# New orders for the middle batches of a fused FFN, attention and FFN kernel: the last layer's second product in steps 6 to 9

## The chip, the cores and the metric

One core of one Trainium2 chip. The time is the device time of one execution in microseconds (us); before is the median of 3 runs. TensorE does matrix products, VectorE and ScalarE read its results from PSUM, GpSimd works on SBUF, SyncE (SP) issues transfers. Each engine runs its own list in order, and semaphores tie the lists together.

## The reference, cut to what matters

```python
x = x + 0.5 * ffn(layernorm(x))            # first FFN ("pre")
x = x + attention(layernorm(x))            # relu attention, and a layernorm of x + out
x = x + 0.5 * ffn(layernorm(x))            # last FFN ("post")

# ffn(x): h = layernorm(x) * gamma + beta; x + 0.5 * (silu(h @ w1 + b1) @ w2 + b2)
#   w1 (128 x 512) and w2 (512 x 128) are dequantised from integers
# attention(x): 16 heads of 8; w = relu(q @ k.T / sqrt(8)); w = w / (sum(w) + 1e-6); (w @ v) @ w_out + b_out
```

x is 8 batches x 512 tokens x 128 features, float32. All products are float32 (q with k as a float32r pair of high and low parts).

## The kernel before, in words

Attention sets the frame: each of the 8 batches has 16 steps (4 groups of 4 heads, by 4 tiles of 128 keys). A step's `step_scores` (S below, L648) writes four 128 x 512 score tiles into four PSUM banks, `scores[i][j]` in the order (0,0), (1,0), (0,1), (1,1). ScalarE takes the relu of i = 0 (L953), VectorE that of i = 1 (L1220), into `probs`, of which there are two sets. `step_values` of the step before (V below, L671) multiplies the relus into one of two `o_bank`s. S of the next step needs the four banks back, so it waits for all relus of this one. In the last batch ScalarE takes three of the four in the steps of THREE_BY_ACT, and in odd steps `scores[1][1]` is replaced by the bank of the pre stage.

Everything else is laid into these steps as fills, by lists written out by hand, one entry a step: PE_ORDER, ACT_ORDER, DVE_ORDER and POOL_ORDER for batches 1 to 6 (POOL_ORDER for 7 too), *_START for batch 0, *_END for batch 7, and *_FIRST and *_LAST around them. TensorE's entries have two parts: the early fills come between S and V, the late ones after V. GpSimd's list has no waits of its own for a step; only its order counts. A name is stage.work@offset, and offset is the batch relative to the one whose steps run: `pre...@1` is work for the next batch, `post...@-1` and `@-2` belong to batches whose attention is over. A name whose batch doesn't exist is left out by `tasks`; so in batch 1 there is no `@-2`.

Two stages, pre and post, have one PSUM bank each, `st.bank`, and each result must be read before the next fill may write it (`next_fill` waits for `st.free`). For a batch the pre bank takes hT (transposed rows), fc1.0 to fc1.3 (each 128 x 512, read by a Silu on ScalarE, L846), fc2 (four fills fc2.0 to fc2.3 that accumulate, read by VectorE as x1), uT, k, q and v. The post bank takes op (attention's output product, read as y), hT, fc1.0 to fc1.3, and fc2, read as out. Between them stand chains through VectorE and GpSimd: x1, x1_stats, x1_stats on GpSimd and u_apply lead to uT; oT.1, den.1, a.1 and aT to op; y, y_stats, y_apply, y_gamma, x2, x2_stats and x_apply to post.hT.

Of the kernel before, what the change touches and what calls it, by code (L numbers as in the profile page):

```python
# [37 lines left out]
POST_FILLS = ["hT", "fc1.0", "fc1.1", "fc1.2", "fc1.3", "fc2"]  # L38
# [28 lines left out]
    (["pre.hT@2"], []),  # L67
]
PE_ORDER = [
    ([], ["post.fc2.0@-2", "pre.fc1.0@1"]),  # L70
    (["post.fc2.1@-2", "post.fc2.2@-2", "post.fc2.3@-2", "pre.fc1.1@1"], []),
    (["pre.fc1.2@1", "post.op@-1"], []),
    (["pre.fc1.3@1"], []),
    (["pre.fc2.0@1"], []),
    ([], ["pre.fc2.1@1"]),
    (["pre.fc2.2@1", "pre.fc2.3@1"], []),
    ([], []),
    ([], []),
    ([], ["post.hT@-1"]),
    ([], []),  # L80
    ([], ["pre.uT@1", "post.fc1.0@-1"]),
    ([], ["pre.k@1", "post.fc1.1@-1"]),
    ([], ["pre.q@1", "post.fc1.2@-1"]),
    ([], ["pre.v@1"]),
    (["post.fc1.3@-1", "pre.hT@2"], []),
]

THREE_BY_ACT = (0, 1, 2, 3, 4, 8, 9, 10, 14)

PE_END = [  # L90
    ([], ["post.fc2.0@-2"]),
    (["post.fc2.1@-2", "post.fc2.2@-2", "post.fc2.3@-2"], []),
    ([], ["post.op@-1"]),
    ([], []),
    ([], []),
    ([], []),
    ([], []),
    ([], []),
    ([], []),
    ([], []),  # L100
# [36 lines left out]
ACT_ORDER = [  # L137
    ["pre.fc1.0@1"],
    ["pre.fc1.1@1"],
    ["pre.fc1.2@1", "post.store@-2", "pre.load_x@2"],  # L140
    ["pre.fc1.3@1"],
    ["post.y_apply@-1"],
    [],
    [],
    [],
    [],
    ["post.hT@-1"],
    [],
    ["pre.uT@1", "post.fc1.0@-1"],
    ["pre.k@1", "post.fc1.1@-1"],  # L150
    ["pre.q@1", "post.fc1.2@-1"],
    ["pre.v@1"],
    ["pre.hT@2", "post.fc1.3@-1"],
]
ACT_END = [
    [],
    [],
    ["post.store@-2"],
    [],
    [],  # L160
    [],
    ["post.y_apply@-1"],
    [],
    [],
    [],
    [],
# [32 lines left out]
]  # L199
DVE_ORDER = [  # L200
    ["oT.1@-1", "den.1@-1"],
    ["a.1@-1", "post.out@-2", "aT@-1"],
    ["post.y@-1", "post.y_stats@-1"],
    [],
    ["pre.x_stats@2"],
    ["post.x2@-1"],
    ["post.x2_stats@-1", "pre.x1@1"],
    [],
    ["pre.x1_stats@1"],
    [],  # L210
    [],
    [],
    ["oT.0", "den.0", "pre.k_lo@1"],
    ["pre.q_lo@1"],
    ["a.0"],
    [],
]
DVE_END = [
    [],
    ["oT.1@-1", "den.1@-1", "a.1@-1", "post.out@-2", "aT@-1"],  # L220
    ["post.y@-1"],
    [],
    ["post.y_stats@-1"],
    [],
    [],
    [],
    ["post.x2@-1"],
    ["post.x2_stats@-1"],
    ["oT.0"],
# [18 lines left out]
    "v_in.0@1", "v_in.1@1", "pre.x1_beta@1", "pre.xr@2"  # L248
]
POOL_ORDER = [  # L250
    [],
    ["post.u_bias"],
    ["post.y_stats@-1", "post.y_gamma@-1"],
    [],
    ["v_in.2", "post.x2_stats@-1", "post.x_apply@-1", "pre.x1_stats@1"],
    [],
    ["pre.u_apply@1"],
    ["pre.x_stats@2"],
    [],
    ["v_in.3", "pre.x_apply@2", "post.xr@-1"],  # L260
    [],
    ["v_in.0@1", "v_in.1@1"],
    ["pre.x1_beta@1"],
    [],
    ["pre.xr@2"],
    [],
]
# [35 lines left out]
def build(nc, x, w_qk, w_v, w_out, fc1_q, fc2_q, fc2_scales, columns, lines, out):  # L303
# [4 lines left out]
    with ExitStack() as ctx:  # L308
        def sb(name, shape, dtype=F32):
            return ctx.enter_context(nc.sbuf_tensor(name, shape, dtype))  # L310
# [4 lines left out]
        def sem(name):  # L315
            return ctx.enter_context(nc.semaphore(name))
# [66 lines left out]
        pre, post = Stage("pre", PRE_FILLS, 2), Stage("post", POST_FILLS, 1)  # L383
# [38 lines left out]
        def emptied(st, h, fill):  # L422

            if fill == "v":
                return pre.free, pre.n_at_edge(f"v.{h}")
            if fill == "q":
                return q_taken, 1
            if st is post and fill.startswith("fc1"):
                return last_silu, int(fill[-1]) + 1
            if st is post and h == 1:  # L430
                return last_free, ("hT", "fc2").index(fill) + 1
            if h == 1 or fill.startswith("fc1"):
                return st.free, len(st.fills) * (0 if st is pre else B - 1) + st.n_at_edge(fill)
            return st.free_a, st.n_at_edge(fill) - (FT if fill != "hT" else 0)

        def free_before(st, b, fill):

            return len(st.fills) * b + st.n(fill) - 1
# [22 lines left out]
        def fc1_bank(st, b, f):  # L461

            return scores[f // 2][:, f % 2, :] if st is post and b == B - 2 else st.bank[:, :]
# [10 lines left out]
        den, rec = sb("den", [P, QB, 2]), sb("rec", [P, QB, 2])  # L474
        a_t = sb("a_t", [P, QB, NP, 2, HD])
        aT = sb("aT", [P, S])
# [21 lines left out]
        v_in, v_in_a = sem("v_in"), sem("v_in_first_half")  # L498
# [8 lines left out]
        op_done, y_done = sem("op_done"), sem("y_done")  # L507
# [59 lines left out]
        def _(pe):  # L567
            mm, transpose = nc.tensor.matmul, nc.tensor.transpose

            def next_fill(st, b, fill):  # L570

                if free_before(st, b, fill) > 0:
                    pe.wait_ge(st.free, free_before(st, b, fill))
# [6 lines left out]
            def transposes(st, b, rows, done):  # L580

                pe.wait_ge(done, b + 1)
                for t in range(TT):
                    last = transpose(st.bank[:, P * t:P * (t + 1)], rows[:, t, :], ident[:, :])  # L584
                last.then_inc(st.full, 1)
# [8 lines left out]
            def by_columns(into, w, tokens):  # L594

                for j in range(HG):
                    part = slice(VW * j, VW * (j + 1))
                    last = mm(into[part, :], w[:, part], tokens, start=True, stop=True)  # L598
                return last

            def ffn(st, b, what):
                if what == "hT":
                    if st is pre and b == 1:

                        pe.wait_ge(*emptied(pre, 0, "v"))
                    else:
                        next_fill(st, b, "hT")
                    if st is post:
                        pe.wait_ge(y_done, b + 1)
                    transposes(st, b, st.h, st.rows)  # L610
                elif what.startswith("fc1"):
                    f = int(what[-1])
                    cols, into = slice(P * f, P * (f + 1)), fc1_bank(st, b, f)
                    if st is post and b == B - 2:

                        pe.wait_ge(probs_done[f // 2][f % 2], STEPS * B)
                        pe.wait_ge(post.free, len(POST_FILLS) * b + post.n("hT"))
                    else:
                        next_fill(st, b, what)
                    by_columns(into, w1_whole[:, cols], st.t[:, :]).then_inc(st.full, 1)  # L620
                elif what.startswith("fc2"):
                    f = int(what[-1])
                    if f == 0 and not (st is post and b == B - 2):
                        next_fill(st, b, "fc2")
                    pe.wait_ge(st.free, len(st.fills) * b + st.n(f"fc1.{f}"))
                    for t in range(TT):
                        last = by_tokens(st.bank, st.y[:, f, :], t, w2[:, f, :], f == 0 and t == 0, f == FT - 1 and t == TT - 1)
                    if f == FT - 1:
                        last.then_inc(st.full, 1)
# [45 lines left out]
            def task(stage, what, b):  # L675
                if stage == "pre":
                    per = len(PRE_FILLS)
                    if what == "uT":
                        next_fill(pre, b, "uT")
                        transposes(pre, b, u1, u_rows)  # L680
                    elif what in ("q", "k"):
                        i = "qk".index(what)
                        next_fill(pre, b, what)
                        by_columns(pre.bank[:, :], wqk[:, i, :], t_u[:, :]).then_inc(pre.full, 1)
                    elif what == "v":
                        pe.wait_ge(pre.free, per * b + pre.n("uT"))
                        next_fill(pre, b, "v")
                        for t in range(TT):
                            last = by_tokens(pre.bank, t_u, t, wv[:, :], True, True)
                        last.then_inc(pre.full, 1)  # L690
                    else:
                        ffn(pre, b, what)
                elif stage == "post":
                    if what == "op":
                        if b == 0:
                            pe.wait_ge(wo_loaded, 16)
                        pe.wait_ge(aT_in, b + 1)
                        if b > 0:

                            pe.wait_ge(post.free, len(POST_FILLS) * b)  # L700
                        for t in range(TT):
                            last = by_tokens(post.bank, aT, t, wo[:, :], True, True)
                        last.then_inc(op_done, 1)
                    else:
                        ffn(post, b, what)
# [746 lines left out]
```

## Time and profile before

| what | us |
|---|---|
| time, median of 3 runs (373.45 to 374.41) | 374.17 |
| the profiled execution: time, span | 373.73, 371.8 |
| TensorE busy | 362.6 (98%) |
| VectorE, ScalarE, GpSimd busy | 271.2, 228.4, 208.2 |
| granted TensorE clock | 1.000 |

Busy is a share of the span. A matmul that waits in the pipeline for a bank counts as busy, so lengths are better read as distances between starts.

### The profile page before, as it was taken

The numbers are of one execution on the slowest core, as the hardware profiler recorded it, in microseconds if no ns is written. First come the engines' busy times: TensorE is split into PE (matmuls) and PEld (weight loads), VectorE is DVE, ScalarE is ACT, GpSimd is POOL, SyncE is SP. The second block draws the span as 40 slices with busy tenths as digits, with TensorE's granted clock in tenths as the row PEclk, the third lists the DMA queues.
The fourth block names the chain that finished last, engine by engine and source line by source line (L and its number), as shares of the span: only waits on it lengthen the run. The fifth ranks groups of instructions, "written<-read, shape, count | busy, mean of one in ns | idle before, by whom it ended". The sixth has DMA issues, their size and how long they took to land.

```text
span 371.8 us, 12667 instructions
## 1 busy us (share of the span) xinstructions
PE 362.6 (98%) x5002; PEld 163.0 (44%) x5002; DVE 271.2 (73%) x666; ACT 228.4 (61%) x416; POOL 208.2 (56%) x440
## 2 busy tenths in 40 slices
PE   8989999999999999999999999999999999999996
PEld 7733423443364324453354433544345533532365
DVE  4766677896669966797767966789667777677673
ACT  3377466756756566556757567565665567588533
POOL 7495146458753697337781587535973384315541
PEclk9999999999999999999999999999999999999999
DMA  7016007300441016300271005410053001700001
GB/s 202 13 28 174 3 3 168 87 3 2 111 119 60 1 28 156 104 2 2 53 178 60 2 2 115 115 58 2 19 143 100 4 0 38 186 35 4 0 4 58
DMA packets 14105, 22.70 MB, mean 61 GB/s; under 512 B 2528, under 2 KB 3808, under 8 KB 14048
## 3 DMA queue, kind: packets, MB, share of 16 engines
q1 hardware_dynamic: 11456, 17.83, 19.8%
q10 hardware_dynamic: 2592, 4.07, 3.3%
q8 instruction: 40, 0.66, 0.7%
q14 instruction: 17, 0.14, 0.1%
HBM read 3.54 MB, written 2.10 MB: 15 GB/s over the span
## 4 chain that ended last, share of the span: by engine, by line
PE 92%; DVE 3%; ACT 2%; issue 2%; POOL 0%; POOLq 0%; DVEq 0%; ACTq 0%
PE o_bank L671 31%; PE scores L648 17%; PE pre_bank L598 10%; PE pre_bank L591 10%; PE post_bank L591 9%; PE post_bank L598 6%; PE scores L598 3%; PE pre_bank L584 2%; PE o_bank L578 2%; DVE probs L1220 1%; PE post_bank L584 1%; ACT probs L953 0%; ACT y_rows L881 0%; PE o_bank L598 0%; DVE post_x L1185 0%
## 5 line engine op out<-in xcount | busy, mean ns | idle before, releaser
L1220 DVE TENSOR_SCALAR probs<-scores 128x512 f32<-128x512 f32 x242 | 155.8, 683 | 59.4 <-PE scores L648 52.9
L953 ACT ACTIVATE probs<-scores 128x512 f32<-128x512 f32 x262 | 141.6, 595 | 64.0 <-PE scores L648 63.9
L671 PE MATMUL o_bank<-probs,v_op 128*32 128x512 f32 x1024 | 135.5, 601 | 0.3 <-DVE probs L1220 0.2
L648 PE MATMUL scores<-q_op,k_op 32*128 32x512 f32 x504 | 76.3, 495 | 1.1 <-ACT probs L953 0.6
L648 PEld LDWEIGHTS scores<-q_op,k_op 32*128 32x128 f32 x504 | 32.1, 181 | 95.3 <-issue 67.7
L671 PEld LDWEIGHTS o_bank<-probs,v_op 128*32 128x32 f32 x1024 | 23.4, 108 | 31.9 <-issue 30.7
L846 ACT ACTIVATE pre_y<-pre_bank,b_sum,col_consts 128x512 f32<-128x512 f32 x28 | 21.8, 779 | 22.9 <-PE pre_bank L598 22.9
L591 PE MATMUL pre_bank<-w,pre_y 128*32 128x128 f32 x960 | 30.7, 274 | 0.0
L598 PE MATMUL pre_bank<-pre_t,w_whole 128*32 128x512 f32 x224 | 29.5, 598 | 0.5 <-ACT pre_y L846 0.5
L591 PEld LDWEIGHTS pre_bank<-w,pre_y 128*32 128x32 f32 x960 | 25.8, 110 | 8.1 <-issue 7.6
L591 PE MATMUL post_bank<-w,post_y 128*32 128x128 f32 x960 | 29.3, 273 | 0.0
L591 PEld LDWEIGHTS post_bank<-w,post_y 128*32 128x32 f32 x960 | 26.2, 110 | 5.8 <-issue 5.3
L1322 POOL TENSOR_TENSOR v_op<-v_rows,v_op 128x128 f32<-128x128 f32 (+1 forms) x33 | 13.6, 423 | 24.5 <-ACT v_rows L867 24.5
L1249 POOL TENSOR_SCALAR norm_x_var<-norm_x_mv 128x4 f32<-128x4 f32 x21 | 4.2, 198 | 39.6 <-DVE norm_x_mv L1009 39.1
L1249 POOL TENSOR_SCALAR norm_y_var<-norm_y_mv 128x4 f32<-128x4 f32 x7 | 1.4, 199 | 43.8 <-DVE norm_y_mv L1009 43.8
L598 PE MATMUL post_bank<-post_t,w_whole 128*32 128x512 f32 x192 | 25.3, 598 | 0.0
L1252 POOL TENSOR_TENSOR norm_x_rs<-norm_x_var,minus_half 128x4 f32<-128x4 f32 x21 | 21.2, 1008 | 1.8
L846 ACT ACTIVATE post_y<-post_bank,b_sum,col_consts 128x512 f32<-128x512 f32 x24 | 18.7, 778 | 5.2 <-PE post_bank L598 5.2
L1383 POOL TENSOR_TENSOR y_rows<-y_rows,rows 128x512 f32<-128x512 f32 x7 | 9.1, 1293 | 16.3 <-ACT y_rows L881 14.2
L1289 POOL TENSOR_TENSOR norm_x_rs<-norm_x_var,minus_half 128x4 f32<-128x4 f32 x16 | 16.2, 1012 | 1.3
L1305 POOL TENSOR_SCALAR pre_xr<-pre_x,norm_x_mix 128x128 f32<-128x128 f32 x32 | 14.8, 476 | 0.8
L598 PE MATMUL pre_bank<-t_u,wqk 128*32 128x512 f32 x112 | 14.6, 594 | 0.1
(168 smaller groups left out, 437.3 us busy)
## 6 DMA issues: line engine op xcount, KB each, us to landing
k_op<-k_parts SPq DMA_DIRECT2D x62, 128.0 KB, 2.6
q_op<-q_parts SPq DMA_DIRECT2D x62, 128.0 KB, 2.8
out_dram<-o_rows ACTq DMA_DIRECT2D x7, 256.0 KB, 2.1
pre_x<-in_x_dram ACTq DMA_DIRECT2D x6, 256.0 KB, 3.1
w_int<-in_L_ffn_fc_q_dram SPq DMA_DIRECT2D x2, 256.0 KB, 4.2
rows<-in_lines_dram ACTq DMA_DIRECT2D x1, 256.0 KB, 6.6
s_rows<-in_L_ffn_fc_scales_dram SPq DMA_DIRECT2D x1, 256.0 KB, 7.5
wqk<-in_w_qk_dram SPq DMA_DIRECT2D x1, 256.0 KB, 7.6
```

What stands on the lines that cost most here:

```text
L584: last = transpose(st.bank[:, P * t:P * (t + 1)], rows[:, t, :], ident[:, :])
L591: last = mm(into[VW * j:VW * (j + 1), P * t:P * (t + 1)], tokens[:, part], w, start=start, stop=stop)
L598: last = mm(into[part, :], w[:, part], tokens, start=True, stop=True)
L648: mm(score_bank(b, s, i, j), k_op[rows, g, P * kt:P * (kt + 1)], q_op[rows, g, :], start=True, stop=True).then_inc(scores_done[i], 1)
L671: last = mm(o_bank[pair][VW * j:VW * (j + 1), :], v_op[:, kt, heads_of(g).start + 2 * j, :], probs[:, s % 2, j, :], start=(odd == 0 and kt ...
L846: activation(st.y[:, f, :], fc1_bank(st, b, f), ACT.Silu, bias=b1_sum[:, f:f + 1], scale=s1_col[:, f:f + 1]).then_inc(st.free, 1)
L953: activation(probs[:, s % 2, 2 * i + j, :], score_bank(b, s, i, j), ACT.Relu).then_inc(probs_done[i][j], 1)
L1220: v.tensor_scalar(probs[:, s % 2, 2 * i + j, :], score_bank(b, s, i, j), 0.0, None, ALU.max).then_inc(probs_done[i][j], 1)
L1252: p.tensor_tensor(norm.rs[:, i, :], norm.var[:, i, :], minus_half[:, i, :], ALU.pow).then_inc(norm.rs_in, 1)
L1289: p.tensor_tensor(norm.rs[:, 0, :], norm.var[:, 0, :], minus_half[:, 0, :], ALU.pow).then_inc(norm.half_in, 1)
L1305: last = p.tensor_scalar(st.xr[:, t, :], st.x(b)[:, t, :], norm.mix[:, 0, t:t + 1], norm.mix[:, 1, t:t + 1], ALU.mult, ALU.add)
L1322: return p.tensor_tensor(v_op[:, ts, heads, first:first + HD], rows, by_one, ALU.mult)
```

## The change

In batches 1 to 6 the four post.fc2@-2 fills go from steps 0 and 1 to steps 6 to 9, and the read of their result (out on VectorE) from step 1 to step 9, its store on ScalarE from step 2 to step 10. pre.fc2.1 goes from late in step 5 to late in step 4, and fc2.2 and fc2.3 from step 6 to step 5. uT goes from late in step 11 to early in step 10, k and q from late in steps 12 and 13 to early in steps 11 and 12, v from step 14 to 13. post.hT@-1 goes from step 9 to 10; post.fc1.0 to fc1.2 stay late in steps 11 to 13, post.fc1.3 goes from step 15 to 14, and hT@2 has step 15 to itself. On VectorE x2_stats, x1 and x1_stats go one step earlier, oT.0 and den.0 from step 12 to 8, a.0 from 14 to 10. In batch 7 post.op stays in step 2, and the fc2@-2 fills go from steps 0 and 1 to steps 3 to 6. GpSimd's list is ordered to match. post.fc2 now waits for y, since the op that shares its bank comes before it, and op waits for the last Silu of the batch before instead of for out.

```diff
 PE_ORDER = [
-    ([], ["post.fc2.0@-2", "pre.fc1.0@1"]),
-    (["post.fc2.1@-2", "post.fc2.2@-2", "post.fc2.3@-2", "pre.fc1.1@1"], []),
+    ([], ["pre.fc1.0@1"]),
+    (["pre.fc1.1@1"], []),
     (["pre.fc1.2@1", "post.op@-1"], []),
     (["pre.fc1.3@1"], []),
-    (["pre.fc2.0@1"], []),
-    ([], ["pre.fc2.1@1"]),
+    (["pre.fc2.0@1"], ["pre.fc2.1@1"]),
     (["pre.fc2.2@1", "pre.fc2.3@1"], []),
-    ([], []),
-    ([], []),
-    ([], ["post.hT@-1"]),
-    ([], []),
-    ([], ["pre.uT@1", "post.fc1.0@-1"]),
-    ([], ["pre.k@1", "post.fc1.1@-1"]),
-    ([], ["pre.q@1", "post.fc1.2@-1"]),
-    ([], ["pre.v@1"]),
-    (["post.fc1.3@-1", "pre.hT@2"], []),
+    ([], ["post.fc2.0@-2"]),
+    ([], ["post.fc2.1@-2"]),
+    ([], ["post.fc2.2@-2"]),
+    (["post.fc2.3@-2"], []),
+    (["pre.uT@1"], ["post.hT@-1"]),
+    (["pre.k@1"], ["post.fc1.0@-1"]),
+    (["pre.q@1"], ["post.fc1.1@-1"]),
+    ([], ["pre.v@1", "post.fc1.2@-1"]),
+    (["post.fc1.3@-1"], []),
+    (["pre.hT@2"], []),
 ]
 PE_END = [
-    ([], ["post.fc2.0@-2"]),
-    (["post.fc2.1@-2", "post.fc2.2@-2", "post.fc2.3@-2"], []),
-    ([], ["post.op@-1"]),
-    ([], []),
-    ([], []),
     ([], []),
     ([], []),
+    ([], ["post.op@-1"]),
+    ([], ["post.fc2.0@-2"]),
+    ([], ["post.fc2.1@-2"]),
+    ([], ["post.fc2.2@-2"]),
+    (["post.fc2.3@-2"], []),
...
 DVE_ORDER = [
     ["oT.1@-1", "den.1@-1"],
-    ["a.1@-1", "post.out@-2", "aT@-1"],
+    ["a.1@-1", "aT@-1"],
     ["post.y@-1", "post.y_stats@-1"],
     [],
     ["pre.x_stats@2"],
-    ["post.x2@-1"],
-    ["post.x2_stats@-1", "pre.x1@1"],
-    [],
+    ["post.x2@-1", "post.x2_stats@-1"],
+    ["pre.x1@1"],
     ["pre.x1_stats@1"],
-    [],
-    [],
-    [],
-    ["oT.0", "den.0", "pre.k_lo@1"],
+    ["oT.0", "den.0"],
+    ["post.out@-2"],
+    ["a.0"],
+    ["pre.k_lo@1"],
     ["pre.q_lo@1"],
-    ["a.0"],
+    [],
+    [],
     [],
 ]
...
                     if f == 0 and not (st is post and b == B - 2):
                         next_fill(st, b, "fc2")
+                        if st is post:
+
+                            pe.wait_ge(y_done, b + 2)
...
-                            pe.wait_ge(post.free, len(POST_FILLS) * b)
+                            pe.wait_ge(post.free, len(POST_FILLS) * (b - 1) + post.n("fc1.3"))
```

## Rows read from the trace of the kernel before

**Rows 1.** The page, part 4: the chain that ended last, by engine.

```profile
PE 92%; DVE 3%; ACT 2%; issue 2%; POOL 0%; POOLq 0%; DVEq 0%; ACTq 0%
```

**Rows 2.** Timeline, TensorE, batch 1: start, length, instructions, [idle before and releaser].

```profile
60.42 0.50 PE L648 MATMUL scores<-q_op,k_op 32*128 32x512 f32 x4
...
62.71 0.51 PE L648 MATMUL scores<-q_op,k_op 32*128 32x512 f32 x4
63.68 1.06 PE L598 MATMUL pre_bank<-pre_t,w_whole 128*32 128x512 f32 x8 [0.46 <-ACT pre_y L846]
...
65.53 0.51 PE L648 MATMUL scores<-q_op,k_op 32*128 32x512 f32 x4
...
68.70 0.51 PE L648 MATMUL scores<-q_op,k_op 32*128 32x512 f32 x4
...
70.99 0.72 PE L648 MATMUL scores<-q_op,k_op 32*128 32x512 f32 x4
...
73.51 0.51 PE L648 MATMUL scores<-q_op,k_op 32*128 32x512 f32 x4
...
82.40 0.51 PE L648 MATMUL scores<-q_op,k_op 32*128 32x512 f32 x4
82.84 1.06 PE L671 MATMUL o_bank<-probs,v_op 128*32 128x512 f32 x8
83.83 0.66 PE L584 MATMUL post_bank<-ident,post_h 128*128 128x128 f32 x4
84.42 0.85 PE L648 MATMUL scores<-q_op,k_op 32*128 32x512 f32 x4
85.20 1.07 PE L671 MATMUL o_bank<-probs,v_op 128*32 128x512 f32 x8
...
101.01 0.51 PE L648 MATMUL scores<-q_op,k_op 32*128 32x512 f32 x4
```

**Rows 3.** Timeline, VectorE, batch 1.

```profile
61.07 1.29 DVE L1220 TENSOR_SCALAR probs<-scores 128x512 f32<-128x512 f32 x2 [1.19 <-PE scores L648]
...
63.50 1.22 DVE L1220 TENSOR_SCALAR probs<-scores 128x512 f32<-128x512 f32 x2
64.64 0.41 DVE L1028 TENSOR_TENSOR a_t<-o_t,rec 128x256 f32<-128x256 f32 x1
65.09 0.71 DVE L1034 STREAM_TRANSPOSE aT<-a_t 128x512 f32<-128x512 f32 x1
...
75.68 0.90 DVE L1074 TENSOR_TENSOR post_x<-y_rows,x_beta 128x512 f32<-128x512 f32 x1 [0.25 <-POOL y_rows L1383]
76.50 1.28 DVE L1220 TENSOR_SCALAR probs<-scores 128x512 f32<-128x512 f32 x2
77.70 0.85 DVE L1000 BATCH_NORM_STATS2 norm_x_stats<-post_x 128x6 f32<-128x128 f32 x4
...
78.89 0.66 DVE L1046 TENSOR_TENSOR x<-pre_bank,pre_xr 128x512 f32<-128x512 f32 x1
79.63 2.72 DVE L1220 TENSOR_SCALAR probs<-scores 128x512 f32<-128x512 f32 x4
82.27 0.86 DVE L1000 BATCH_NORM_STATS2 norm_x_stats<-x 128x6 f32<-128x128 f32 x4
...
83.47 1.25 DVE L1220 TENSOR_SCALAR probs<-scores 128x512 f32<-128x512 f32 x2
```

**Rows 4.** Timeline, GpSimd, batch 1: the last step of u_apply.

```profile
85.67 1.76 POOL L1280 TENSOR_SCALAR u<-x,norm_x_rs,norm_x_shift 128x128 f32<-128x128 f32 x4 [0.21 <-POOL norm_x_shift L1256]
```

**Rows 5.** Timeline, TensorE: first scores of batches 6 and 7; step 6 and V(7) of batch 7.

```profile
275.22 0.50 PE L648 MATMUL scores<-q_op,k_op 32*128 32x512 f32 x4
...
318.25 0.51 PE L648 MATMUL scores<-q_op,k_op 32*128 32x512 f32 x4
...
331.69 0.76 PE L648 MATMUL scores<-q_op,k_op 32*128 32x512 f32 x4
...
336.33 1.06 PE L671 MATMUL o_bank<-probs,v_op 128*32 128x512 f32 x8
```

More of the change, by code:

```diff
@@ L139 @@
     ["pre.fc1.1@1"],
-    ["pre.fc1.2@1", "post.store@-2", "pre.load_x@2"],
+    ["pre.fc1.2@1", "pre.load_x@2"],
     ["pre.fc1.3@1"],
@@ L146 @@
     [],
-    ["post.hT@-1"],
     [],
[L149 to L153, printed above, removed]
+    ["post.store@-2", "pre.uT@1", "post.hT@-1"],
+    ["pre.k@1", "post.fc1.0@-1"],
+    ["pre.q@1", "post.fc1.1@-1"],
+    ["pre.v@1", "post.fc1.2@-1"],
+    ["post.fc1.3@-1"],
+    ["pre.hT@2"],
 ]
@@ L157 @@
     [],
-    ["post.store@-2"],
+    [],
     [],
@@ L162 @@
     ["post.y_apply@-1"],
-    [],
+    ["post.store@-2"],
     [],
@@ L205 @@
     ["pre.x_stats@2"],
-    ["post.x2@-1"],
-    ["post.x2_stats@-1", "pre.x1@1"],
-    [],
+    ["post.x2@-1", "post.x2_stats@-1"],
+    ["pre.x1@1"],
     ["pre.x1_stats@1"],
-    [],
-    [],
-    [],
-    ["oT.0", "den.0", "pre.k_lo@1"],
-    ["pre.q_lo@1"],
-    ["a.0"],
+    ["oT.0", "den.0"],
+    ["post.out@-2"],
+    ["a.0"],
+    ["pre.k_lo@1"],
+    ["pre.q_lo@1"],
+    [],
+    [],
     [],
@@ L219 @@
     [],
-    ["oT.1@-1", "den.1@-1", "a.1@-1", "post.out@-2", "aT@-1"],
+    ["oT.1@-1", "den.1@-1", "a.1@-1", "aT@-1"],
     ["post.y@-1"],
@@ L225 @@
     [],
-    [],
+    ["post.out@-2"],
     ["post.x2@-1"],
@@ L250 @@
 POOL_ORDER = [
-    [],
+    ["v_in.2"],
     ["post.u_bias"],
@@ L254 @@
     [],
-    ["v_in.2", "post.x2_stats@-1", "post.x_apply@-1", "pre.x1_stats@1"],
     [],
-    ["pre.u_apply@1"],
     ["pre.x_stats@2"],
-    [],
-    ["v_in.3", "pre.x_apply@2", "post.xr@-1"],
+    ["post.x2_stats@-1", "post.x_apply@-1", "v_in.3"],
+    ["pre.x1_stats@1", "pre.u_apply@1"],
+    [],
+    ["pre.x_apply@2"],
+    ["post.xr@-1"],
     [],
+    ["pre.x1_beta@1"],
     ["v_in.0@1", "v_in.1@1"],
-    ["pre.x1_beta@1"],
-    [],
     ["pre.xr@2"],
```

## The prediction

> **What bounds the kernel now.** I read the chain that ended last first: nine tenths of the span is TensorE, so what counts is the order and the gaps of TensorE's stream [rows 1]. The busy share says little about gaps, because a score matmul that waits for its PSUM bank is drawn long and counts as busy. So I read TensorE's timeline and take every length as the distance from one start to the next [rows 2]; batch 1 holds every pattern that the change uses.
> A step is S (four score matmuls), V (eight value matmuls) and its fills. S takes 0.44 (82.40 to 82.84), V alone 0.99 (to 83.83), a turn ("hT", "uT") 0.59 (to 84.42), a step with one fill 2.29 (68.70 to 70.99), with two 3.17 (65.53 to 68.70); so one more fill is 0.88 [rows 2]. Early or late in the step costs TensorE the same.
> Two things stretch this. (a) The last score matmul takes the bank that VectorE's second relu has read: in batch 1's step 10 that relu ends at 83.47 + 1.25 = 84.72 and V starts at 85.20, 0.48 later [rows 2, 3]. (b) Each stage has one bank for its fills: in step 1 fc1.1 starts 0.97 after S (62.71 to 63.68) instead of 0.44, released by the Silu of fc1.0, a late fill of the step before; step 1 is 2.82 [rows 2]. In the later batches of before the three post.fc2 fills stand between the two, and cover that wait.
> VectorE's own pace: its relus start 0.65 after S (60.42 to 61.07), a pair ends after 1.28 but makes room for the next instruction after 1.20 (76.50 to 77.70); x2_stats 1.19, x1 0.74, x1_stats 1.20, x2 0.82 (75.68 to 76.50), oT with den 63.50 - 61.07 - 1.20 = 1.23, a 0.45, aT 0.71 [rows 3].
>
> **The change, a middle batch (2 to 5).** No instruction is added or dropped; only orders and two waits that are met long before (y_done for post.fc2, and the op wait, which now asks for the Silu of fc1.3 instead of out). SP's list and the DMAs are unchanged; the store moves to step 10 on ScalarE, behind its relus, and ScalarE has room for it. What counts is how long the steps are in the new order.
> Steps 0 to 3 now read exactly as batch 1's do in before, where post.fc2 does not exist: 70.99 - 60.42 = 10.57 [rows 2], wait (b) of 0.53 included; it used to be hidden. Step 4: as 70.99 to 73.51, 2.52 (VectorE's y and y_stats are the same neighbours, so their 0.22 wait stays), plus fc2.1, 0.88: 3.40. So step 5 starts at T = 13.97. Step 5 has two fills, 3.17; steps 6 to 9 one each, 9.16; so the uT of step 10 can start at T + 12.77 (with S). Step 10 then takes 0.59 + 0.99 + 0.59 = 2.17, steps 11 to 13 two fills each, 9.51. Step 14 has fc1.3 early behind fc1.2 late in step 13: wait (b) again, since it is the same pair on the other stage's bank, so 2.82. Step 15 is 0.44 + 0.59 + 0.99 = 2.02. Sum 13.97 + 12.77 + 2.17 + 9.51 + 2.82 + 2.02 = 43.26. Before, batches 2 to 5 took (275.22 - 101.01) / 4 = 43.55 [rows 2, 5]. Gain 0.29 each, 1.16 for four: the stalls in the empty steps 7, 8 and 10 go, and two waits of 0.53 come.
> Does VectorE keep up? After relu(5) it is free at T + 0.65 + 1.20 = T + 1.85; x2 to 2.67, x2_stats 3.86, relu(6) 5.06, x1 5.80. relu(7) waits for its scores until T + 6.11, free 7.31; x1_stats 8.51; relu(8) 9.71; oT.0 and den.0 10.94; relu(9) ends 12.22, and 0.48 on is 12.70: in time for 12.77, with 0.07 to spare. out, a.0, k_lo and q_lo lie in steps with 0.4 or more to spare.
> Does GpSimd? u's last apply ends at 85.67 + 1.76 = 87.43, 5.16 after x1_stats starts at 82.27 [rows 3, 4]. Here x1_stats starts at T + 7.31, so u is there at T + 12.47, 0.30 before uT.
> These are narrow, and no row shows this neighbourhood. From below the cost is zero, from above 0.3 a batch (that the last hand-over falls behind by as much as its spare). I take 0.1, nearer the rows, for each of batches 1 to 6: 0.5 to 0.6 in all.
>
> **Batch 1** is in the middle table too, but its post.fc2@-2 does not exist: steps 6 to 9 are empty, four in a row, where before only 7, 8 and 10 were. There VectorE sets the pace, one piece behind the other: relu(6) to 5.06, x1 5.80, relu(7) 7.00, x1_stats 8.20, relu(8) 9.40, oT.0 and den.0 10.63, relu(9) ends 11.91, + 0.48 = T + 12.39. So the batch takes 43.26 - 0.38 = 42.88, though TensorE has four fills less to do; before it took 101.01 - 60.42 = 40.59 [rows 2]. Loss 2.29. This is the largest term: before, those fills sat in steps 0 and 1, whose length was TensorE's own, so leaving them out shortened the batch; now they sit where VectorE's work (oT.0 and den.0 moved up from step 12) fills the time anyway.
>
> **Batch 6** has no hT@2: its step 15 is empty, 1.43. 42.67 against 318.25 - 275.22 = 43.03 [rows 5]: gain 0.36.
>
> **Batch 7.** From its first S (Z). relu(15) ended 1.93 after S(15), so V(15) starts 0.48 later, at Z + 0.98, and S(1) at Z + 1.97. VectorE does one relu there (free at Z + 3.22), then oT.1 with den.1, a.1 and aT: 1.23 + 0.45 + 0.71, ending at Z + 5.61. op in step 2 needs aT, and TensorE is there by Z + 4.7 to 5.2 (the three fills that covered this chain in step 1 are gone), so it waits and starts at 5.65; behind it wait the scores of step 3, and so both relu engines. S(3) at 6.62, three one-fill steps, S(6) at 13.49. In step 6 y_apply delays ScalarE's relus: V(7) starts 336.33 - 331.69 = 4.64 after S(6), so Z + 18.13, against 336.33 - 318.25 = 18.08 before [rows 5]. The fill in step 6 now hides what the wait at op costs: +0.05. Bounds -0.5 and +1.0, since which of the three relus of ScalarE ends last in steps 0 to 2 is no row here. The tail is the same.
>
> **Sum.** 2.29 - 1.16 - 0.36 + 0.05 = +0.82, with the 0.1 a batch for tight hand-overs +1.4; I take +1.3. The profiled execution has 373.73 us for its span of 371.8, so 375.0; it lay 0.44 under the median of 374.17, which gives 375.5 for the median.
>
> **A page against the rows.** The Trainium skill, VectorE: DVE Perf Modes, section "The DRAIN you can't avoid", says that the next VectorE operation does not start until the pipe of the last is empty. The row of a relu pair is 1.28 long and its follower starts after 1.20 [rows 3]; the trace does not agree, so the sum goes by start distances.
>
> **Rivals.** (1) Faster: wait (b) does not come. If the Silu of a late fill freed the bank before S is over, step 14 of batches 1 to 6 and step 1 of batches 2 to 6 would be 0.53 shorter, 11 x 0.53 = 5.8, and the time 369.7. It decides from about 5 of the 11: then the time falls below 373.1. For it: in before no middle batch shows the wait. Against: there nothing asks for the bank so soon, and the one place that does shows it [rows 2]. Chance 0.12, with a smaller loss in batch 1 in it.
> (2) VectorE's chain or u runs late in all middle batches: the 0.07 and 0.30 are used up, den takes longer beside GpSimd. 0.3 to 0.5 for each of batches 2 to 6: 377.3. For it: the spare is less than a tenth of one relu pair. Against: each duration repeats in before. Chance 0.2. To it belongs what the full-length spacing would do as a mechanism: follower 0.08 later for each of four relu pairs is 0.3 in batch 1 and 0.25 in each of five others, +1.6, 377.1; this is what the page's rule would bring; chance 0.03 of the 0.2.
> (3) Nothing to see: batch 1 loses its 2.29, but the others gain 0.4 to 0.5, and no tight hand-over costs anything: 374.2. Chance 0.13.
> The forecast has 0.55, and its own range is 374.6 to 376.4.
>
> **How the numbers follow.** 0.3%, 1.12 us, is about what a measurement of this kernel can tell from no change, so slower begins at 375.3. The forecast lies close above it: of its 0.55 I give 0.33 to slower, 0.22 to the same. With rival 2 slower has 0.53, with rival 3 the same 0.35, faster 0.12. The range 374.0 to 377.3 leaves out most of rival 1 and the ends of 2 and of batch 7's bound.
>
> **What would show it.** Batch 1 near 43 from first S to first S, batches 2 to 5 near 43.3; in them fc1.1 of step 1 and fc1.3 of step 14 released by a Silu 0.97 after S; S(7) to S(10) of batch 1 drawn 0.7 to 1.2 long behind VectorE's relu; op of batch 7 released by aT. It is wrong if batch 1 stays near 41, or if middle batches come under 42.8 or over 43.7.

## The result and the profile after

The changed kernel takes 375.0 us (median of 13 runs, 374.21 to 375.75), the kernel before 373.87 beside it (13 runs, 373.4 to 374.42): ratio 1.0031, 95% interval 1.0022 to 1.0040. It is slower by 0.2 to 0.4%; the forecast of 375.5 was 0.5 too high, its direction right. As a difference the forecast was +1.3, and +1.13 was measured. The profiled execution has a span of 373.1 us against 371.8.

The chain that ended last has less TensorE and more of what TensorE waits for:

```profile
PE 86%; DVE 6%; ACT 3%; issue 2%; DMA 1%; POOL 0%; SPq 0%; ACTq 0%; DVEq 0%; POOLq 0%
```

The timeline of TensorE in batch 1, in the same columns as [rows 2]:

```profile
60.46 0.51 PE L651 MATMUL scores<-q_op,k_op 32*128 32x512 f32 x4 [0.50 <-DMA q_op<-q_parts]
...
62.75 0.51 PE L651 MATMUL scores<-q_op,k_op 32*128 32x512 f32 x4
63.72 1.07 PE L598 MATMUL pre_bank<-pre_t,w_whole 128*32 128x512 f32 x8 [0.46 <-ACT pre_y L849]
...
71.04 0.73 PE L651 MATMUL scores<-q_op,k_op 32*128 32x512 f32 x4
...
74.44 0.51 PE L651 MATMUL scores<-q_op,k_op 32*128 32x512 f32 x4
...
79.05 1.05 PE L651 MATMUL scores<-q_op,k_op 32*128 32x512 f32 x4
...
81.02 0.86 PE L651 MATMUL scores<-q_op,k_op 32*128 32x512 f32 x4
...
82.81 1.45 PE L651 MATMUL scores<-q_op,k_op 32*128 32x512 f32 x4
...
85.19 1.44 PE L651 MATMUL scores<-q_op,k_op 32*128 32x512 f32 x4
86.57 0.64 PE L584 MATMUL pre_bank<-ident,u 128*128 128x128 f32 x4
...
98.17 0.51 PE L651 MATMUL scores<-q_op,k_op 32*128 32x512 f32 x4
99.14 1.07 PE L598 MATMUL post_bank<-post_t,w_whole 128*32 128x512 f32 x8 [0.46 <-ACT post_y L849]
...
101.00 0.50 PE L651 MATMUL scores<-q_op,k_op 32*128 32x512 f32 x4
...
103.01 0.51 PE L651 MATMUL scores<-q_op,k_op 32*128 32x512 f32 x4
```

The reader is to see three things. The batch takes 103.01 - 60.46 = 42.55, where it took 40.59 [rows 2]. Four scores in a row, from 79.05 on, are drawn 0.86 to 1.45 long where 0.5 is normal: TensorE waits in steps 7 to 10, behind VectorE's relus (steps 6 to 9 have no fill). And two fills are released by a Silu, each 0.97 after its S: fc1.1 at 63.72 and, new, fc1.3 of the post stage at 99.14, which makes step 14 101.00 - 98.17 = 2.83 long.

VectorE and GpSimd in the same stretch, to be held against [rows 3, 4]:

```profile
76.27 0.68 DVE L1077 TENSOR_TENSOR post_x<-y_rows,x_beta 128x512 f32<-128x512 f32 x1
76.99 0.87 DVE L1003 BATCH_NORM_STATS2 norm_x_stats<-post_x 128x6 f32<-128x128 f32 x4
...
79.46 0.68 DVE L1049 TENSOR_TENSOR x<-pre_bank,pre_xr 128x512 f32<-128x512 f32 x1
80.06 1.28 DVE L1223 TENSOR_SCALAR probs<-scores 128x512 f32<-128x512 f32 x2
81.25 0.86 DVE L1003 BATCH_NORM_STATS2 norm_x_stats<-x 128x6 f32<-128x128 f32 x4
82.15 0.38 DVE L1012 BATCH_NORM_AGGREGATE norm_x_mv<-norm_x_stats 128x2 f32<-128x6 f32 x4
82.45 1.26 DVE L1223 TENSOR_SCALAR probs<-scores 128x512 f32<-128x512 f32 x2
83.62 0.71 DVE L1021 STREAM_TRANSPOSE o_t<-o_bank 128x512 f32<-128x512 f32 x1
84.36 0.19 DVE L1024 TENSOR_SCALAR den<-o_t 128x32 f32<-128x32 f32 x1
84.59 0.35 DVE L1026 RECIPROCAL rec<-den 128x32 f32<-128x32 f32 x1
84.86 2.58 DVE L1223 TENSOR_SCALAR probs<-scores 128x512 f32<-128x512 f32 x4
```

```profile
84.66 1.76 POOL L1283 TENSOR_SCALAR u<-x,norm_x_rs,norm_x_shift 128x128 f32<-128x128 f32 x4 [0.21 <-POOL norm_x_shift L1259]
```

VectorE has no gap: relu(9) starts at 84.86 (the row holds two pairs, 1.29 each) and ends 1.29 later, and 0.48 on is 86.63; uT starts at 86.57. But u too is ready only at 84.66 + 1.76 = 86.42. Two chains end within 0.2 of each other.

All batches, from first S to first S (each a difference of such rows; the last column is from batch 7's first S to its last):

| kernel | batch 1 | 2 to 5, each | 6 | 7 to last S |
|---|---|---|---|---|
| before | 40.59 | 43.54 to 43.57 | 43.03 | 29.59 |
| changed | 42.55 | 43.24 to 43.28 | 42.67 | 30.46 |
| difference in all | +1.96 | -1.16 | -0.36 | +0.87 |

That is +1.31; the spans differ by 1.3. Two more differences of these two executions cancel. The first S of all starts at 21.45 instead of 21.92, and batch 0, whose lists are the same in both kernels, takes 39.01 instead of 38.50, since the first S of batch 1 waits 0.50 for the transfer of q_op (the row at 60.46). Of the twelve traces five have this wait, 0.31 to 0.60 long, and seven do not; what decides it is open. The tail, from the last S to the end, is 23.91 against 23.96.

Batch 7: VectorE ahead of op, and ScalarE around the store, then the scores that wait (TensorE):

```profile
323.78 0.71 DVE L1037 STREAM_TRANSPOSE aT<-a_t 128x512 f32<-128x512 f32 x1
```

```profile
335.58 1.07 ACT L956 ACTIVATE probs<-scores 128x512 f32<-128x512 f32 x2
337.34 0.34 ACTq L889 DMA_DIRECT2D out_dram<-o_rows  x1
337.78 2.56 ACT L956 ACTIVATE probs<-scores 128x512 f32<-128x512 f32 x5 [1.13 <-DVE o_rows L1087]
```

```profile
318.73 1.06 PE L651 MATMUL scores<-q_op,k_op 32*128 32x512 f32 x4
...
324.54 1.08 PE L591 MATMUL post_bank<-wo,aT 128*32 128x128 f32 x32 [0.45 <-DVE aT L1037]
...
337.13 1.07 PE L674 MATMUL o_bank<-probs,v_op 128*32 128x512 f32 x8
338.43 0.98 PE L651 MATMUL scores<-q_op,k_op 32*128 32x512 f32 x3 [0.23 <-ACT probs L956]
```

op waits for aT, as foretold. What was not foretold is the 1.13 before ScalarE's relus of step 8: its list has the store in step 7, the store waits for out, and out is behind VectorE's relus.

### The profile page after: what moved, and what is told of

Read it like the earlier page. It is cut to its first block, busy times and chain, and to the rows that moved or that the text cites. A ratio compares the mean times of both kernels' runs of the same rounds, so it can differ in the third digit from the quotient of the medians.

```text
span 373.1 us, 12667 instructions
## 1 busy us (share of the span) xinstructions
PE 358.3 (96%) x5002; PEld 161.3 (43%) x5002; DVE 268.8 (72%) x666; ACT 228.4 (61%) x416; POOL 208.4 (56%) x440
## 3 DMA queue, kind: packets, MB, share of 16 engines
HBM read 3.54 MB, written 2.10 MB: 15 GB/s over the span
## 4 chain that ended last, share of the span: by engine, by line
PE 86%; DVE 6%; ACT 3%; issue 2%; DMA 1%; POOL 0%; SPq 0%; ACTq 0%; DVEq 0%; POOLq 0%
PE o_bank L674 28%; PE scores L651 13%; PE pre_bank L598 11%; PE pre_bank L591 10%; PE post_bank L591 9%; PE post_bank L598 6%; PE scores L598 3%; DVE probs L1223 3%; PE pre_bank L584 2%; PE o_bank L578 2%; ACT pre_y L849 1%; ACT post_y L849 1%; PE post_bank L584 1%; DMA q_op<-q_parts 1%; DVE o_t L1021 1%
## 5 line engine op out<-in xcount | busy, mean ns | idle before, releaser
L651 PE MATMUL scores<-q_op,k_op 32*128 32x512 f32 x504 | 72.9, 495 | 1.4 <-DMA q_op<-q_parts 0.5
L651 PEld LDWEIGHTS scores<-q_op,k_op 32*128 32x128 f32 x504 | 29.2, 181 | 88.2 <-issue 71.0
L674 PEld LDWEIGHTS o_bank<-probs,v_op 128*32 128x32 f32 x1024 | 25.5, 109 | 36.3 <-issue 33.5
L591 PE MATMUL post_bank<-w,post_y 128*32 128x128 f32 x960 | 31.5, 273 | 0.0
```

Source lines behind the costliest of these rows:

```text
L591: last = mm(into[VW * j:VW * (j + 1), P * t:P * (t + 1)], tokens[:, part], w, start=start, stop=stop)
L651: mm(score_bank(b, s, i, j), k_op[rows, g, P * kt:P * (kt + 1)], q_op[rows, g, :], start=True, stop=True).then_inc(scores_done[i], 1)
L674: last = mm(o_bank[pair][VW * j:VW * (j + 1), :], v_op[:, kt, heads_of(g).start + 2 * j, :], probs[:, s % 2, j, :], start=(odd == 0 and kt ...
```

## The experiments

Ratios are to the kernel before on the same chip. The parts act in different batches, so the trace tells them apart better than the time does.

**Batch 1 in the order of before.**

```diff
+PE_SECOND, ACT_SECOND, DVE_SECOND, POOL_SECOND = the four lists of the kernel before
-def of_batch(b, start, order, end):
-    return start if b == 0 else end if b == B - 1 else order
+def of_batch(b, start, second, order, end):
+    return start if b == 0 else second if b == 1 else end if b == B - 1 else order
...
-            for beside in POOL_ORDER:
+            for beside in POOL_SECOND if b == 1 else POOL_ORDER:
```

> Batch 1 alone gets the order lists of the kernel before; all else is the changed kernel. Theory: in batch 1 the moved fills do not exist, and steps 6 to 9 run at VectorE's pace; the trace of the changed kernel has 42.55 us from the first S of batch 1 to that of batch 2, before had 40.59. So batch 1 returns to 40.6 and the time falls by 1.96, from 375.0 to 373.0, which is 0.8 under before (373.87). Rival: the batch is long for what comes into it from batch 0 (q and k transfers, values), not for its own order; then the time stays within 0.5 of 375.0. Rival 2: the time saved is waited for again in batch 2; then batch 2 grows above 43.25.

Measured 373.08 us, ratio 0.9988 (0.9976 to 1.0000). Its first scores of batches 1 and 2 (TensorE):

```profile
60.35 0.50 PE L724 MATMUL scores<-q_op,k_op 32*128 32x512 f32 x4
...
100.94 0.51 PE L724 MATMUL scores<-q_op,k_op 32*128 32x512 f32 x4
```

Batch 1 takes 40.59 again, and batches 2 to 6 keep their 43.23 to 43.28 and 42.65. The loss is batch 1's own order. By the trace the middle order alone is a gain of 1.5 in batches 2 to 6; the time is only 0.5 under before, since batch 7 keeps its loss.

**Batch 7 in the order of before.**

```diff
 (PE_END, ACT_END and DVE_END of the kernel before)
-                        if st is post:
+                        if st is post and b < B - 3:
                             pe.wait_ge(y_done, b + 2)
...
-                            pe.wait_ge(post.free, len(POST_FILLS) * (b - 1) + post.n("fc1.3"))
+                            pe.wait_ge(post.free, len(POST_FILLS) * (b if b == B - 2 else b - 1)
+                                       + (0 if b == B - 2 else post.n("fc1.3")))
```

> Batch 7 alone gets the lists of before, with the two waits that belong to that order. In the changed kernel its last S comes 30.47 us after its first, before 29.60. Theory: the order of batch 7 is worth 0.87 (wait for aT at op, and the store), so 374.1. Rival: the long first S (0.99) that comes from batch 6's empty last step makes the loss; batch 7 keeps it in this run, so the time would fall by less than 0.4.

Measured 374.59, ratio 1.0029 (1.0018 to 1.0040). Batch 7 takes 30.14 to its last S, 0.32 less than in the changed kernel, not 0.87. The rival holds: batch 7's first S waits in this kernel too (V 0.98 after S, as in the changed kernel 0.99), because batch 6 now ends in an empty step.

```profile
318.73 1.04 PE L651 MATMUL scores<-q_op,k_op 32*128 32x512 f32 x4
319.71 1.06 PE L674 MATMUL o_bank<-probs,v_op 128*32 128x512 f32 x8
```

So 0.87 splits: 0.55 by that first S, which belongs to the order of batch 6, and 0.32 by batch 7's own order.

**The store one step later.**

```diff
 ACT_END = [
...
     ["post.y_apply@-1"],
-    ["post.store@-2"],
     [],
+    ["post.store@-2"],
```

> In batch 7 the store of out goes from step 7 to step 8 of ScalarE's list. In the changed kernel ScalarE's relus of step 8 start 1.13 late, released by VectorE's out; V(8) and the steps behind it are late. Theory: the wait in front of the store costs the 0.5 that batch 7 lost between V(7) and its last S (12.06 against 11.52 before), so 374.5. Rival: out itself takes VectorE's time before relu(8); then nothing changes, 375.0.

Measured 374.43, ratio 1.0020 (1.0010 to 1.0030), which overlaps the changed kernel's; the trace decides. ScalarE no longer stops:

```profile
335.72 1.07 ACT L956 ACTIVATE probs<-scores 128x512 f32<-128x512 f32 x2
337.02 0.60 ACT L956 ACTIVATE probs<-scores 128x512 f32<-128x512 f32 x1 [0.23 <-PE scores L651]
```

The gap of 1.13 is 0.23, and batch 7 takes 29.89 instead of 30.46. So the place of the store costs 0.57. With it out of the way the new order of batch 7 is 0.25 better than the old one of the experiment above (30.14); 0.57 less 0.25 is the 0.32 found there.

**op in step 3 of batch 7** (with the store later).

```diff
 PE_END = [
     ([], []),
     ([], []),
-    ([], ["post.op@-1"]),
-    ([], ["post.fc2.0@-2"]),
+    ([], []),
+    ([], ["post.op@-1"]),
+    ([], ["post.fc2.0@-2"]),
...
 (fc2.1 to fc2.3 and y one step later, out behind x2, the store one step later)
```

> The changed kernel with the store later, and in batch 7 op in step 3 instead of 2, fc2@-2 in steps 4 to 7, y one step later, out and the store after x2. Theory: op in step 2 waits 0.62 for aT, with the scores and both relu engines behind it; in step 3 aT is there, so batch 7 goes from 29.89 to 29.3 and the time to 373.8. Rival: y, y_apply and x2 are late then, and a later step takes it back; 374.4 or more.

Measured 374.63, ratio 1.0022 (1.0010 to 1.0034); batch 7 takes 30.03, against 29.89 with op in step 2. The time is in the rival's range, but not for its reason. op no longer waits, but S of step 3 does:

```profile
324.37 0.50 PE L651 MATMUL scores<-q_op,k_op 32*128 32x512 f32 x1
325.46 0.50 PE L651 MATMUL scores<-q_op,k_op 32*128 32x512 f32 x2 [0.59 <-DVE probs L1223]
```

VectorE's one relu of step 2 is queued behind oT.1, den.1, a.1 and aT. The 2.4 us of VectorE work stayed in its empty step, and a wait for VectorE stayed too, at S instead of at op. That the wait would go with this work was not tried.

**fc1.3 late in step 14.**

```diff
-    (["post.fc1.3@-1"], []),
+    ([], ["post.fc1.3@-1"]),
     (["pre.hT@2"], []),
```

> post.fc1.3@-1 goes from early to late in step 14 of batches 1 to 6, nothing else. Theory of the one bank: early, it waits for the Silu of fc1.2 until 0.97 after S; late, it starts 1.32 after S, when the bank is free. Step 14 goes from 2.82 to 2.29, six times 0.53 = 3.2: 371.8. Rival: the Silu is then later and ScalarE's relus of step 15 or the copy of hT come late; S of step 0 or fc1.0 takes back up to 0.5 a batch, and the time stays within 1 of 375.0.

Measured 371.60, ratio 0.9948 (0.9936 to 0.9960). TensorE in batch 3, steps 14 and 15:

```profile
183.06 0.50 PE L651 MATMUL scores<-q_op,k_op 32*128 32x512 f32 x4
183.49 1.07 PE L674 MATMUL o_bank<-probs,v_op 128*32 128x512 f32 x8
184.37 1.04 PE L598 MATMUL post_bank<-post_t,w_whole 128*32 128x512 f32 x8
185.34 0.51 PE L651 MATMUL scores<-q_op,k_op 32*128 32x512 f32 x4
```

The step is 2.28, and the middle batches 42.71 to 42.74: the 0.53 is gone in each and nothing takes it back. (Batch 6, with its empty last step, falls by 0.40, and the first step of batch 7 by 0.13.) One entry moved from the early to the late side of the same step is worth 3 us, and makes this kernel faster than before by 0.4 to 0.6%.

**The other fills late too.**

```diff
     ([], ["pre.fc1.0@1"]),
-    (["pre.fc1.1@1"], []),
-    (["pre.fc1.2@1", "post.op@-1"], []),
-    (["pre.fc1.3@1"], []),
-    (["pre.fc2.0@1"], ["pre.fc2.1@1"]),
+    ([], ["pre.fc1.1@1"]),
+    ([], ["post.op@-1", "pre.fc1.2@1"]),
+    ([], ["pre.fc1.3@1"]),
+    ([], ["pre.fc2.0@1", "pre.fc2.1@1"]),
```

> Batches 1 to 6: besides post.fc1.3 (step 14), pre.fc1.1, fc1.2, fc1.3 and fc2.0 go from early to late in steps 1 to 4, op goes ahead of fc1.2. Theory of the one bank: step 1 loses its 0.53 wait as step 14 did, and with op later in step 2 VectorE's y no longer... delays relu(3), or still does: y can start 0.3 after relu(2) instead of 0.5 behind it, and S(4) keeps 0 to 0.22 of its wait. So 0.53 x 6 more than fc1.3 alone, and up to 0.22 x 6: 371.6 - 3.2 - 0.7 = 367.7, between 367.1 and 368.4; middle batches 42.0 to 42.2. Rival: with all fills late VectorE's chain (0.07 spare at step 10) or ScalarE's Silus, which now come before each relu pair, become the bound and give back 0.3 or more a batch: over 369.5.

Measured 370.41, ratio 0.9906 (0.9889 to 0.9922): a miss for the theory, and in the rival's range, though the wait that takes the gain back is not one that the rival names. Step 1 lost its 0.53, but the middle batches came down by 0.16 only, to 42.55 to 42.58. S(4) keeps its 0.22, since y_stats still stands ahead of relu(3), and S(2) is 0.38 over. VectorE's den.1 is 0.83 long here. The lines of VectorE and GpSimd (batch 3, step 0):

```profile
148.40 0.83 DVE L1024 TENSOR_SCALAR den<-o_t 128x32 f32<-128x32 f32 x1
149.26 0.35 DVE L1026 RECIPROCAL rec<-den 128x32 f32<-128x32 f32 x1
149.53 1.22 DVE L1223 TENSOR_SCALAR probs<-scores 128x512 f32<-128x512 f32 x2
```

```profile
147.51 0.42 POOL L1325 TENSOR_TENSOR v_op<-v_rows,v_op 128x128 f32<-128x128 f32 x1
147.89 1.28 POOL L1377 TENSOR_TENSOR u_bias<-u,rows 128x512 f32<-128x512 f32 x1
```

den should take 0.19; it ends at 149.23, when GpSimd's u_bias (149.17) has ended. In the changed kernel it meets only the end of u_bias in these batches, and takes 0.28 to 0.31.

**oT.0 and den.0 back to step 12, in batch 1 alone.**

```diff
+DVE_SECOND = DVE_ORDER with oT.0, den.0 in step 12 and a.0 in step 14, for b == 1
```

> The changed kernel, but in batch 1 alone oT.0 and den.0 go back from step 8 to step 12 and a.0 to step 14. VectorE's chain from step 5 to relu(9) is then 1.2 shorter. If that chain alone sets when step 10's uT starts, batch 1 falls from 42.55 to 41.3 and the time by 1.2. If u sets it nearly as much (in the changed kernel GpSimd's last u ends at 86.42 and uT starts at 86.57), the wait only moves from S to uT and batch 1 falls by 0.1 to 0.2: 374.8.

Measured 374.68, ratio 1.0020 (1.0011 to 1.0030), and in the trace batch 1 is 42.51 instead of 42.55. TensorE at step 10:

```profile
84.45 0.50 PE L670 MATMUL scores<-q_op,k_op 32*128 32x512 f32 x4
85.82 0.63 PE L603 MATMUL pre_bank<-ident,u 128*128 128x128 f32 x4 [0.86 <-POOL u L1302]
```

VectorE's chain, which my prediction gave as the cause, is 1.1 to 1.2 shorter, and the batch is as long: the wait now carries u's name. The two are nearly equal bounds, and taking one away shows the other. What is common to both is x1_stats: VectorE starts it 20.79 after the batch's first S in the changed kernel (at 81.25) and 20.78 after it here. That an earlier x1_stats would shorten the batch is argued, not shown.

**All together.** Batch 1 as before with its fc1 and fc2.0 fills late, late fills in batches 2 to 6, the store later.

```diff
 (the edits above: the late fills, the lists of before for b == 1 with theirs late, the store)
```

> All at once: late fills in batches 2 to 6, in batch 1 the order of before with fc1 and fc2.0 late, the store of batch 7 one step later. Theory: the parts add, since each acts in its own batch or step: batch 1 39.9, batches 2 to 5 42.0 each, batch 6 41.4, batch 7 29.9 to its last S; 365.3. Rival: the parts share their gain (the next bound in a batch comes up); over 367.

Measured 368.07, ratio 0.9839 (0.9825 to 0.9854). Batch 1 is 40.05, batches 2 to 5 42.54 to 42.59, batch 6 42.09, batch 7 29.73. The parts add: batch 1 is the 40.59 of the order of before less the 0.54 of fc1.1's wait, the middle batches are those of the kernel with late fills, and batch 7 is 0.55 shorter than there, as with the store alone. The time is over the rival's 367, but not because parts share their gain: the 365.3 that I expected had 42.0 for a middle batch, without den's wait and S(4)'s.

**GpSimd out of den's way.**

```diff
 POOL_ORDER = [
     ["v_in.2"],
-    ["post.u_bias"],
+    [],
...
-    ["post.xr@-1"],
+    ["post.xr@-1", "pre.xr@2"],
     [],
     ["pre.x1_beta@1"],
-    ["v_in.0@1", "v_in.1@1"],
-    ["pre.xr@2"],
+    ["v_in.0@1", "v_in.1@1", "post.u_bias@1"],
+    [],
 (batch 1's list likewise, with x1_beta ahead of v_in.0 and v_in.1; its own u_bias stays in step 1)
```

> The combined kernel, with GpSimd's list alone changed: xr@2 right behind xr@-1, and u_bias of the next batch right behind v_in.1@1, so that GpSimd is idle when VectorE does den.1 in step 0. In the combined kernel den.1 takes 0.82 to 0.83 in batches 2 to 6 instead of 0.19, and ends as GpSimd's u_bias ends; relu(1) is late and S of step 2 is 0.38 long over. Theory: den waits for GpSimd's instruction; with GpSimd idle it takes 0.2, S(2) comes down to 0.44 to 0.49, and five batches lose 0.35 each: 368.1 - 1.8 = 366.3. Rival: den waits for something else (the result of the transpose, the semaphore); den stays at 0.8 and the time within 0.5 of 368.1. Rival 2: the earlier xr delays v_in.0 or x1_beta, and V(0) or x1 waits: over 368.

Measured 366.92, ratio 0.9810 (0.9794 to 0.9826). GpSimd is idle from 185.44 to 194.86, and VectorE's den.1 of batch 4 in that stretch:

```profile
188.31 0.19 DVE L1097 TENSOR_SCALAR den<-o_t 128x32 f32<-128x32 f32 x1
```

den waits for GpSimd's instruction: with GpSimd idle it takes 0.19. Batches 2 to 5 take 42.17 to 42.21, 0.34 to 0.40 less. The time fell by 1.15 and not by 1.8, because of batch 1. GpSimd's list is still full there at that place, and the same thing happened to another operation. VectorE, then GpSimd:

```profile
64.87 1.40 DVE L1104 TENSOR_TENSOR a_t<-o_t,rec 128x256 f32<-128x256 f32 x1
```

```profile
64.70 1.28 POOL L1391 TENSOR_TENSOR pre_xr<-pre_xr,b_quarter 128x512 f32<-128x512 f32 x1
```

a.1 takes 0.41 when alone. It cost 0.63 at op, and batch 1 is 40.70 here. In the combined kernel a.1 begins at 64.03, ahead of the same instruction of GpSimd at 64.30, and takes 0.46. The order turned because TensorE's first S of batch 1 waited for q_op's transfer here (0.32) and not there. In all five traces with that wait a.1 takes 1.02 to 1.41, in the other seven 0.41 to 0.46.

**y_stats one step later.**

```diff
 DVE_ORDER = [
...
-    ["post.y@-1", "post.y_stats@-1"],
-    [],
+    ["post.y@-1"],
+    ["post.y_stats@-1"],
```

> As the kernel with GpSimd's list changed, and y_stats goes from step 2 to step 3 of VectorE's list, behind relu(3), in batches 1 to 6. Theory: relu(3) no longer waits behind y_stats, and S(4) loses its 0.22: six times, 1.3 less, 365.0. Rival: y_stats is 1.7 later; y_apply then meets relu(5) on ScalarE and y_gamma comes after relu(5) on VectorE, so x2 and the chain behind it, which has 0.07 to 0.1 to spare, run late and give back 0.2 to 0.4 a batch: 366.0 to 367.5.

Measured 368.81, ratio 0.9869 (0.9855 to 0.9884): a miss for the theory. S(4) lost its 0.22, and S(7) now waits 0.42, since x2 and the chain behind it are late; middle batches take 42.39 to 42.41, 0.2 more than without the move. The rival was right in kind. The time went up by 1.9. Of this the traces show 1.0 in batches 2 to 6 (0.2 each), 0.7 in batch 1 (41.41 against 40.70) and 0.3 in batch 0, whose end waits 0.60 for q_op's transfer instead of 0.32.

## Why the prediction was right

Point by point, by its own steps.

- Middle batches: computed 43.26, measured 43.24 to 43.28. The starts read in batch 1 of before, put together in the new order, are right to 0.02. Both waits of kind (b), at fc1.1 and fc1.3, came 0.97 after S, and the experiment with fc1.3 late showed that the one bank is the cause. The rival that this wait does not come (369.7) is out.
- The 0.1 a batch for narrow hand-overs did not exist: nothing was late. This term, 0.5 of the forecast, was wrong. The spare was also larger than the 0.07 computed, since x2 takes 0.72 in the new order and not 0.82.
- Batch 1: loss 2.29 computed, 1.96 measured. uT started at 86.57 - 74.44 = 12.13 after T instead of 12.39. The size was off because VectorE's x2 and x1 took less room there (76.99 - 76.27 = 0.72 and 80.06 - 79.46 = 0.60) than the 0.82 and 0.74 of [rows 3]. The mechanism was half told: u is as late as VectorE's chain. The prediction did not work u out for this place; by its own steps u would have had 12.39 - 7.00 - 5.16 = 0.23 to spare. The scores of steps 9 and 10 are drawn 1.45 and 1.44 long, where it said 1.2 at most.
- Batch 6: -0.36 computed and measured.
- Batch 7: +0.05 computed, +0.87 measured, inside its bounds of -0.5 to +1.0. The first S was right (0.99 against 0.98), and op at 324.54 - 318.73 = 5.81 against 5.65. V(7) came 18.40 after the first S, not 18.13, and 18.08 before: +0.32. The other 0.55 comes behind V(7) and is the store, an edit that I had costed only for the middle batches, where it stands one step after out; in batch 7 it stands in the same step as out. The step that failed is the sentence that ScalarE has room for the store: ScalarE waited 1.13 there, and the batch is 0.57 shorter with the store one step later.
- Sum: 0.82 without the hand-overs and 1.3 with them; the traces have 1.31, the medians 1.13. That the sum is so near is luck: batch 7's error (+0.82) and batch 1's (-0.33) happen to make up the 0.5 that the hand-overs did not take. Of the 0.5 by which 375.5 was too high, 0.3 is the kernel before, which took 373.87 here and 374.17 when the prediction was made.
- The Trainium skill, VectorE: DVE Perf Modes, section "The DRAIN you can't avoid": the prediction used its sentence that the next operation does not start until the pipe is empty, but the section also says that a next operation that is not held starts earlier. In the changed kernel the relu pair at 82.45 is drawn 1.26 long and its follower starts at 83.62, 1.17 after it began. The trace does not agree with the first sentence alone; by the second it would be a pair whose follower is not held, which no run here tests.

## What to carry to other kernels

In a stream that is full, moving work gains only what the gaps were worth, and each move must be priced at every place where the pattern it makes exists: the first and last iterations miss some of the fills, and there the same order was 5% slower (42.55 against 40.59). With one buffer between producer and reader, count the distance from the end of one fill to the start of the next: here late after late is free, and late then early costs 0.53 each time. Where two chains end within 0.2 of each other, shortening one moves the wait and not the time.

## What the hardware showed beyond that

VectorE and GpSimd get in each other's way, and the profile shows it as a long instruction and not as a wait. den (0.19 alone) took 0.83 and ended 0.06 after GpSimd's u_bias; with GpSimd idle it took 0.19 again. a (0.41 alone) took 1.40 where an instruction of GpSimd had begun before it, and ended at 66.27, 0.29 after that one's end at 65.98. Who began first matters: where a began first it took 0.46. The kernel before has such a place too: in its batch 6 den takes 1.08 and ends 0.05 after an instruction of GpSimd, and step 13 is 3.36 long instead of 3.15.

The Trainium skill, SBUF — State Buffer, section "Who interferes with whom", says that a VectorE instruction in a two-port mode contends with GpSimd, that whichever issues first keeps the shared ports for its whole length while the other is blocked, and that a VectorE instruction with two SBUF inputs contends with a GpSimd instruction that reads SBUF. The trace agrees for den and a in when they end; that their kinds are the ones named was not tried by itself.

In one trace TensorE's clock fell in the steps of batch 1 that have no fill. In the profiled execution of the kernel with late fills (stretches of 4 us; the columns are length, busy of each engine, granted clock, DMA share and GB/s):

```profile
80.00:84.00 4.00, 3.90 (x28) 1.23 (x24) 3.90 (x15) 2.17 (x4) 3.39 (x10) 1.00 0.00 0
84.00:88.00 4.00, 3.91 (x24) 1.46 (x16) 3.01 (x6) 1.69 (x3) 3.86 (x9) 0.72 0.01 4
88.00:92.00 4.00, 4.00 (x32) 1.48 (x32) 1.51 (x3) 2.14 (x4) 3.71 (x9) 0.86 0.00 0
```

0.72 is part of the time at 1.2 instead of 2.4 GHz; from 86 to 89 the granted clock is 0.50. Before it, TensorE had waited in the scores of steps 7 to 10, which the busy column hides (3.90 of 4), and step 10 took 5.06 instead of 3.54.

That these waits are the cause is not shown. The trace of the changed kernel has the same waits at a clock of 1.00, and all its 13 runs have a mean clock of 1.000. Of the 69 runs of kernels with four such steps in batch 1, two have a mean clock of 0.995: this execution, and one of 12 of the kernel with op in step 3, which took 376.2 against a median of 374.63. No recorded run of the kernel before, or of those with batch 1 in its order, has less than 0.999. Two cases are too few to tell the kinds apart.
